# One mask product per score bank in place of two, in the last attention of a four-layer block

## What is computed

```python
q = heads(tgt @ Wq + bq) / sqrt(D_K)          # 16 heads of 16
k = heads(memory @ Wk + bk)
v = heads(memory @ Wv + bv)
scores = einsum('bhqd,bhkd->bhqk', q, k)
scores = where(mask[:, None, :, :], -1e18, scores)
attn = softmax(scores, axis=-1)
ctx = einsum('bhqk,bhkd->bhqd', attn, v)
x = x + tanh(g) * (ctx.reshape(b, -1, 256) @ Wo + bo)
```

## Time and profile before

| | |
|---|---|
| median of 3 runs | 1635.72 us (1634.01 to 1636.18) |
| the profiled execution's own time | 1638.06 us |
| its span, first to last instruction | 1636.3 us |
| mean granted TensorE clock, share of full speed | 0.916 |
| TensorE (PE) busy | 1386.8 us, 85% |
| VectorE (DVE) busy | 1240.5 us, 76% |
| ScalarE (ACT) busy | 772.5 us, 47% |
| GpSimd (POOL) busy | 337.0 us, 21% |

### The profile page before, as it was taken

One profiled execution on the slowest core, in us unless ns is written; L12 is line 12 of the kernel. 1 busy time (PEld: TensorE's weight loads), 2 busy tenths in 40 slices (PEclk: granted clock), 3 DMA queues, 4 the chain that ended last, 5 costly groups with the idle time before them and its releaser, 6 DMA issues.

```text
span 1636.3 us, 25886 instructions
## 1 busy us (share of the span) xinstructions
PE 1386.8 (85%) x9890; PEld 1266.5 (77%) x9890; DVE 1240.5 (76%) x2386; ACT 772.5 (47%) x1318; POOL 337.0 (21%) x278
## 2 busy tenths in 40 slices
PE   4897997798995599999399459968998999999995
PEld 4786895586883599999379358966886888999995
DVE  5696778777896589997379779976886857888773
ACT  4445442113455266666355442325445225676673
POOL 2241001000000157764100000000000013454342
PEclk9898998799998599998699879988998999999997
DMA  4232100000002478886300000000002016777784
GB/s 139 91 104 89 45 1 1 1 0 10 1 1 110 150 211 233 244 224 174 124 1 1 7 0 1 1 10 1 1 1 104 1 65 233 233 214 220 219 241 116
DMA packets 44926, 148.23 MB, mean 91 GB/s; under 512 B 11651, under 2 KB 22582, under 8 KB 35062
## 3 DMA queue, kind: packets, MB, share of 16 engines
q1 hardware_dynamic: 28886, 122.04, 21.9%
q0 software_dynamic: 15936, 24.78, 7.8%
HBM read 126.03 MB, written 22.87 MB: 91 GB/s over the span
## 4 chain that ended last, share of the span: by engine, by line
PE 56%; DVE 26%; ACT 8%; issue 5%; DMA 2%; POOLq 1%; SPq 1%; POOL 0%; ACTq 0%; DVEq 0%
PE PS L307 37%; PE PS L1005 6%; PE PS L966 3%; PE PS L989 3%; DVE RA L1624 2%; PE PS L1240 1%; DVE RA L1693 1%; ACT Y L225 1%; ACT RA L1617 1%; DVE FA L1661 1%; PE PS L998 1%; DVE RA L297 1%; PE PS L982 1%; DVE RA L1673 1%; POOLq L2764 1%
## 5 line engine op out<-in xcount | busy, mean ns | idle before, releaser
L307 PE MATMUL PS<-RA 128*128 128x256 f32 (+3 forms) x6204 | 942.7, 311 | 74.9 <-DVE RA L397 16.2
L307 PEld LDWEIGHTS PS<-RA 128*128 128x128 f32 x6204 | 859.5, 197 | 130.3 <-issue 34.5
L1551 POOL DMA_INDIRECT sum_rows<-Y,KT x78 | 158.6, 2033 | 193.1 <-ACT Y L1592 162.2
L271 POOL TENSOR_TENSOR rstd<-vareps,neghalf 128x4 f32<-128x4 f32 x36 | 36.8, 1023 | 707.2 <-DVE vareps L208 330.0
L1005 PE MATMUL PS<-VBF,FA 128*128 128x136 f32 x1024 | 136.1, 287 | 4.4 <-ACT FA L771 4.2
L1540 POOL DMA_INDIRECT Y<-normed_rows,KT x78 | 89.8, 1151 | 219.7 <-DVE KT L1333 158.5
L1005 PEld LDWEIGHTS PS<-VBF,FA 128*128 128x128 f32 x1024 | 124.8, 192 | 10.3 <-ACT FA L771 6.8
L771 ACT ACTIVATE FA<-PS 128x1024 f32<-128x1024 f32 x64 | 65.7, 1027 | 103.9 <-PE PS L966 103.9
L1570 ACT ACTIVATE FA<-PS,unit_bias 128x256 f32<-128x256 f32 (+1 forms) x184 | 71.7, 445 | 78.2 <-PE PS L307 65.4
L1624 DVE TENSOR_TENSOR RA<-FA,RA 128x2048 fp32r<-128x2048 f32 x46 | 105.2, 2288 | 4.4 <-ACT RA L1584 3.7
L1693 DVE TENSOR_TENSOR RA<-FA,RA 128x1024 fp32r<-128x1024 f32 (+1 forms) x46 | 80.9, 1759 | 24.8 <-ACT RA L1617 24.8
(11 more groups left out here) (295 smaller groups left out, 1874.9 us busy)
## 6 DMA issues: line engine op xcount, KB each, us to landing
FA<-in_eup SPq DMA_DIRECT2D x46, 1024.0 KB, 7.0
FA<-in_edown SPq DMA_DIRECT2D x23, 1024.0 KB, 6.3
FA<-in_edown SPq DMA_DIRECT2D x23, 512.0 KB, 4.1
FA<-in_fside SPq DMA_DIRECT2D x16, 512.0 KB, 3.6
sum_rows<-X SPq DMA_DIRECT2D x2, 2048.0 KB, 7.4
normed_rows<-Y SPq DMA_DIRECT2D x2, 2048.0 KB, 10.2
fp_rows<-FA POOLq DMA_DIRECT2D x6, 352.0 KB, 6.8
FA<-fp_rows SPq DMA_DIRECT2D x1, 2112.0 KB, 11.9
```

Of the source, the lines that this page charges most:

```text
L307: ins = pe.matmul(dst, stat(a, k), mov(b, k), start=(first and n == 0), stop=(last and n == len(todo) - 1))
L1551: pool.indirect_dma_start(out=sum_rows, in_=rows_out[p][:, t, :], in_offset=None, compute_op=ALU.add, out_offset=bass.IndirectOffsetOnAxis ...
```

## The change

The constant becomes -2^60 (about -1.15e18), which the format holds exactly. `neg` has one part in place of two, VectorE's L866 and its wait go, TensorE waits for a `neg_ready` count of one, and each score bank gets one mask product in place of two.

```diff
@@ -605,8 +605,9 @@
-            neg = rview(19968, 2, NT, S2)
+            neg = rview(19968, NT, S2)
             ident_r = rview(22016, P)
+            MASKED = -2.0 ** 60
             neg32 = fview(5120, NT, S2)
@@ -745,7 +746,7 @@
                     if masked:
-                        act.activation(neg[:, 0], mask[:, :, :], ACT.Copy, scale=-1e18)
+                        act.activation(neg, mask[:, :, :], ACT.Copy, scale=MASKED)
                         act.activation(ident_r, ident[:, :], ACT.Copy).then_inc(neg_ready, 1)
@@ -861,10 +862,6 @@
                     queries_lo(2)
-                    if masked:
-                        dve.wait_ge(neg_ready, 1)
-                        dve.scalar_tensor_tensor(neg[:, 1], mask[:, :, :], -1e18, neg[:, 0].bitcast(F32), ALU.mult, ALU.subtract
-                                                 ).then_inc(neg_ready, 1)
                     queries_lo(3)
@@ -953,7 +950,7 @@
                 if masked:
-                    pe.wait_ge(neg_ready, 2)
+                    pe.wait_ge(neg_ready, 1)
@@ -977,11 +974,10 @@
                         if masked:
-                            for m in range(2):
-                                for r in range(ROWTILES):
-                                    pe.matmul(PS[:, 2 * p + r, :].rearrange("p (h s) -> p h s", s=S2), ident_r,
-                                              neg[:, m, t:t + 1, :].to_broadcast([P, HC, S2]), start=(m == 0), stop=False,
-                                              skip_group_check=True)
+                            for r in range(ROWTILES):
+                                pe.matmul(PS[:, 2 * p + r, :].rearrange("p (h s) -> p h s", s=S2), ident_r,
+                                          neg[:, t:t + 1, :].to_broadcast([P, HC, S2]), start=True, stop=False,
+                                          skip_group_check=True)
```

## The result

The median fell from 1635.78 to 1631.98 us (20 runs of each): ratio 0.9976, 95% interval 0.9969 to 0.9984, so 3.9 us faster (2.6 to 5.1). The forecast was 7.1 us, and 1631.98 lies above its range. Between 55 and 70% of what was forecast arrived, and the question is where the rest went.

What follows compares the result with a forecast made beforehand. TensorE was taken to bound the last attention's slots; 0.61 (start) + 6.58 (fourteen tiles) - 0.10 (end) = 7.1 us saved, giving a median of 1628.6 us, range 1626.2 to 1631.6.

Steps and rivals of the forecast that it cites:

- Price of a product, 0.47 us a tile: Last attention's slots: two mask products fewer save 2 x 0.235 us of TensorE per tile, 6.58 us over fourteen tiles.
- Its sign of being right, starts 0.235 apart in the pair: Profile after: the two mask products left in a pair would start 0.235 us apart.
- VectorE has 0.52 us of slack and absorbs the folding slots: Last attention's slots: VectorE needs 4.67 us against 5.19; folding slots overrun by 0.29, costing TensorE nothing.
- Rival A: VectorE closes the slot; its folding overruns reach TensorE and 1.0 to 1.5 us come back: 1629.6 to 1630.1; chance 0.11.
- ScalarE's loop stays open: Slots: ScalarE's copy of transposed probabilities does not limit; the L966 to L1005 interval falls to 2.63 us, above 2.15.
- Start, 0.61: Stage start: without L866's wait (0.14 us) and with 0.47 off tile 0, the first slot starts 0.61 us earlier.
- End, 0.10 given back: Stage end, slot 14: VectorE is late after slot 13's statistics, giving back 0.1 us (bounds 0 and 0.3).
- The sum of all this, 7.1: Whole stage: 0.61 + 6.58 - 0.10 = 7.1 us saved.
- Tile 1's saving lies in TensorE's gap behind that and is worth nothing: Ahead of the first slot: tile 1's shorter mask work only falls into TensorE's gap, gaining 0.
- All later stages start from the barrier at the end of this one and move as a whole: After the last attention: everything behind the barrier shifts earlier by the same 7.1 us.
- the shift against the clock's changes: Later stages, 7 us earlier: one 3.4 us low-clock stretch more or less, 1.7 us either way.
- Rival D: Slots: less TensorE work per slot drops the granted clock; eight low stretches there would give 1642 us; chance 0.02.

Runs made afterwards that it cites:

- filled kernel: Changed kernel with tile 1's mask products issued five times instead of once, filling TensorE's pause; median 1629.75 us over 24 runs.
- a3_double: Changed kernel with each mask product issued twice, the second anew from zero; 1637.40 us, ratio 1.0007 to the kernel before.
- b1_before: The kernel before the change, unedited, run again against the same kernel; 1638.99 us, ratio 1.0014.
- c4_double_from2: Changed kernel with one mask product per bank for tiles 0 and 1, two for the fourteen others; 1640.92 us, ratio 1.0038 to the kernel before.
- a4_nomask: Changed kernel with no mask products, the scores starting their sums themselves; 1628.69 us, ratio 0.9953 to the kernel before.
- c3: Changed kernel, pause left open, with the mask products of tiles 2 to 6 doubled; 1633.41 us, ratio 0.9988 to the kernel before.
- b2_again: The changed kernel once more, unedited; 1632.42 us, ratio 0.9972 to the kernel before.

## Why the prediction was wrong

By its own steps:

- *Price of a product, 0.47 us a tile*: right. Slots of 5.19 us, and 4 x 0.47 more when four tiles are doubled (88.27 - 86.40 = 1.87). Its sign of being right, starts 0.235 apart in the pair, was not: they are 0.32 apart (1156.07 and 1156.39), and the scores follow 0.33 behind, which are the two outer gaps of its own working. An estimate from the Trainium skill's 131 ns per product (TensorE: Matmul & The Clock Gate, Back-to-back issue gap) gives 5.40, which the trace does not bear out.
- *VectorE has 0.52 us of slack and absorbs the folding slots*: right; its waits in plain slots are 0.48, and TensorE waited in none of slots 5, 9 and 13. Rival A is out.
- *ScalarE's loop stays open*: right, from L963 at 1155.28 to L1001 at 1157.90 is 2.62 us, 2.63 expected.
- *Start, 0.61*: 0.75. From the first of the 24 query products to L904 it is 7.21 us (1122.97 to 1130.18), 7.96 before. The wait for L866 had cost 0.19 (5.77 against 5.58 to the first mask product), above my bound of 0.18, and from there to the scores of tile 0 it is 0.54 us in place of 1.10 (1129.01 - 1127.91 before), so that its pair was worth 0.56 and not 0.47.
- *End, 0.10 given back*: 0.07, from L307 of slot 13 to that of slot 14: 4.88 us against 4.81 before. Right.
- The sum of all this, 7.1, is what the filled kernel's slots part shows: 7.2.
- *"Tile 1's saving lies in TensorE's gap behind that and is worth nothing"*: this is the step that failed. It was worth less than nothing. The pause grew from 1.72 to 2.18 us, behind it the clock was low for 3.4 us, and 87.86 - 86.40 = 1.5 us of the saving went. With the pause filled or as before, the clock held in all seven profiles.
- *"All later stages start from the barrier at the end of this one and move as a whole"*: this failed too. The section behind the slots cost the changed kernel about 1.2 us more. I had named the shift against the clock's changes as 1.7 us either way and taken its mean as zero; for the changed kernel's shift it had one sign in all four profiles. This is the weaker of the two: in the first profiles of both kernels the section is 21.41 and 21.30, and the 1.2 us come from the other profiles of before and a3_double.

Together 7.2 - 1.5 - 1.2 = 4.5 us, against 5.0 as the mean of four comparisons and 3.9 in the first. The 0.6 us between this and the first result is inside its interval; the comparison of two equal kernels was off by more. That the sum meets the mean so closely is in part luck. It leaves out the rest of the execution, which from the section's end on took 390.2, 393.6 and 388.6 us in before, b1_before and a3_double and 388.5 to 389.8 in the changed kernel, and which no run here resolves; the profiled executions as a whole are 6.1 us apart (spans of 1636.6 and 1630.5 on average). Rival D had the clock right and the reason and the place wrong: it expected the clock to fall inside the slots because each holds less work, and it fell behind the pause ahead of them, with slots of before (c4_double_from2) as with shorter ones. I looked for low clock in the slots, found 1.00 in the unmasked attention from 855 on, and stopped there. Had I read the same trace of before where that attention's slots begin, in the timeline of TensorE and the busy time by stretch, I would have seen that it can fall there:

```profile
830.52 1.97 PE L966 MATMUL PS<-ident,FA 128*128 128x128 f32 x8 [3.43 <-ACT FA L779]
...
834.00 3.23 PE L1005 MATMUL PS<-VBF,FA 128*128 128x136 f32 x16
```
```profile
829.47:836.30 6.83, 5.78 (x30) 5.23 (x31) 2.26 (x2) 2.96 (x3) 0.00 (x0) 0.50 0.01 2
```

There the pause is 3.43 us, its transposes take the same 1.97 us and the clock is 0.50. The masked attention of before was the one with the shorter pause, because its mask products filled it (without them, in a4_nomask, it is 3.43 us as well). But the same trace shows a limit to this reading. Attention 1 has the same pause, and there the clock held, in 13 of the 17 profiles; in four, a3_double among them, it fell. The timelines of TensorE in before and in a3_double:

```profile
421.53 1.09 PE L966 MATMUL PS<-ident,FA 128*128 128x128 f32 x8 [3.43 <-ACT FA L779]
```
```profile
420.73 1.97 PE L963 MATMUL PS<-ident,FA 128*128 128x128 f32 x8 [3.43 <-ACT FA L780]
```

## What to carry to other kernels

When an edit takes work from TensorE, look where that work stood in front of a wait: there it is not free to remove, since it may have been what kept the clock up for the dense part behind. Compare such a pause with the longer and shorter ones of the same trace and the granted clock behind each, and do so in more than one profile, since equal pauses can differ in what follows. Where the clock is at risk, try a few products that compute nothing new, in the pause and off the chain: here eight of them took 1.5 us off the stage. And for an effect of 0.2%, compare lengths of parts in several profiles: the slots part repeated to 0.3 us where medians of equal kernels differed by 2.9. Not every part does: the section behind the slots differed by 1.35 us between two profiles of before.

## What the runs showed that was not expected

In the last attention a difference of 0.46 us in one pause goes with the clock: after 1.69 to 1.72 us of idle time it held (five profiles: two of before, a3_double, two with two products for tiles 0 and 1), after 2.17 to 2.18 us it fell (six: four of the changed kernel, c3 and c4). With the pause filled to 0.32 us it held in five, though the first transposes came 20.0 to 20.4 us behind the clock's last rise, where they come in the changed kernel too (19.9 to 20.5); so there the idle time made the difference. For the pause of 1.7 us the two are not separated, since its transposes came later, 20.5 to 21.0 us behind the rise.

The length of a pause alone is no rule. In attention 1 it was 3.42 or 3.43 us in all 17 profiles; the clock held in the thirteen in which the transposes came 15.20 to 15.31 us behind its last rise, and fell in the four in which they came 15.13 to 15.17 us behind. So the outcome goes with the place of a pause as well, here within 0.1 us. The Trainium skill (TensorE: Matmul & The Clock Gate, the section on why this matters for kernels) advises no idle gaps of more than about 3 us between bursts; here 2.2 us, behind a few microseconds of dense products, was enough six times of six, and 3.4 us was not enough thirteen times of seventeen. The trace does not agree with it as a bound, on either side.

Second, the low stretch did not come at random: in the four profiles of the changed kernel it began 0 to 0.6 us behind the first transposes of the slots (of b2_again 1133.77 and 1134.32), although the executions had reached that point at times 3.5 us apart (their slots parts begin at 1121.8 to 1125.3).
